# A two-layer transformer on one core: the transfers of the turned maxima are issued by ScalarE instead of SyncE

## The reference

```
xn = layernorm(x);  x = x + attention0(xn) + ffn0(xn)     # layer 0
xn = layernorm(x);  x = x + attention1(xn) + ffn1(xn)     # layer 1

scores = q k^T      (32 heads of 16 columns, causal, -inf above the diagonal)
weights = softmax(scores * 0.25);  context = weights v;  attention = context Wo + bo
ffn(x)  = (act(x gate_w) * (x up_w)) down_w               # 1792 wide, then 1376 wide
```

## Time and profile before

| | |
|---|---|
| median of 3 runs | 811.23 us (810.88 to 814.6) |
| the profiled execution | 813.03 us, of which 811.1 us are the span from its first to its last instruction |
| granted TensorE clock, mean | 0.993 |
| PE, PEld | 769.3 us (95%), 589.6 us (73%) |
| DVE, ACT, POOL | 520.8 us (64%), 406.4 us (50%), 403.7 us (50%) |
| DMA | 113.79 MB, 55.3% of 16 engines' span, all issued by SP (669 issues, 128 of them for the maxima) |
| chain that ended last | PE 79%, DVE 7%, DMA 6%, SP 4%, issue 2%, ACT 2% |

### The profile page before, as it was taken

How to read it: one execution, slowest core, us unless ns; L and a number is a source line. 1 busy time by engine, 2 the same in 40 slices (tenths; PEclk the granted TensorE clock), 3 DMA queues, 4 the chain that set the end, 5 groups by cost and what they waited for, 6 DMA issues and landing times.

```text
span 811.1 us, 19165 instructions
## 1 busy us (share of the span) xinstructions
PE 769.3 (95%) x7172; PEld 589.6 (73%) x7172; DVE 520.8 (64%) x1536; ACT 406.4 (50%) x756; POOL 403.7 (50%) x549
## 2 busy tenths in 40 slices
PE   7899999999999999999979989997989989999996
PEld 4788888877777876687657767674766767787764
DVE  7777765677765678766578668515776857765323
ACT  2253455466655556545535564452364635645630
POOL 4344555555755554455435544357454644555631
PEclk9999999999999999999999999999899999999999
DMA  6557347463736363637784373289628586833331
GB/s 220 135 190 165 116 145 159 115 150 101 159 110 141 117 142 108 141 103 155 206 159 161 87 149 100 68 194 216 168 100 166 157 173 195 150 118 108 96 103 66
DMA packets 71932, 113.79 MB, mean 140 GB/s; under 512 B 21144, under 2 KB 21144, under 8 KB 71832
## 3 DMA queue, kind: packets, MB, share of 16 engines
q1 hardware_dynamic: 71840, 112.57, 55.3%
HBM read 87.04 MB, written 25.43 MB: 139 GB/s over the span
## 4 chain that ended last, share of the span: by engine, by line
PE 79%; DVE 7%; DMA 6%; SPq 4%; issue 2%; ACT 2%; POOL 0%; DVEq 0%; ACTq 0%
PE bank L1347 63%; PE bank L1491 6%; PE bank L1475 4%; PE bank L1457 4%; SPq L940 3%; DMA w_raw<-weights_in 2%; DVE bank L1292 2%; DMA k_op<-qk_scratch 1%; DMA m_scratch<-m_rows 1%; DMA q_op<-m_scratch 1%; DVE gate L1254 1%; DVE xt_lo L1221 1%; ACT gate L1099 1%; PE bank L1367 1%; DMA x<-x_in 1%
## 5 line engine op out<-in xcount | busy, mean ns | idle before, releaser
L1045 POOL TENSOR_TENSOR w_lo<-w_raw,w_hi 128x512 fp32r<-128x512 f32 x202 | 264.2, 1319 | 124.6 <-ACT w_hi L1087 122.0
L1292 DVE CUSTOM_DVE_ANT_0 bank<-bank,causal 128x128 f32<-128x128 f32 (+3 forms) x512 | 237.0, 520 | 76.1 <-PE bank L1457 75.3
L1067 POOL TENSOR_SCALAR_AFFINE_SELECT p<-p 128x256 f32<-128x256 f32 (+1 forms) x320 | 118.2, 370 | 256.5 <-ACT p L1080 248.9
L1080 ACT ACTIVATE p<-bank 128x512 f32<-128x512 f32 x320 | 173.6, 597 | 119.2 <-PE bank L1475 118.7
L1347 PE MATMUL bank<-xt_hi,w_hi 64*128 64x512 f32 x1008 | 206.0, 400 | 13.5 <-DVE h L1263 4.8
L1347 PE MATMUL bank<-xt_lo,w_hi 64*128 64x512 f32 x1008 | 201.6, 391 | 0.0
L1347 PE MATMUL bank<-xt_hi,w_lo 64*128 64x512 f32 x1008 | 201.3, 391 | 0.0
L1087 ACT ACTIVATE w_hi<-w_raw 128x512 fp32r<-128x512 f32 x202 | 120.8, 631 | 33.5 <-DMA w_raw<-weights_in 17.0
L1347 PEld LDWEIGHTS bank<-xt_hi,w_hi 64*128 64x128 f32 x1008 | 98.4, 187 | 38.8 <-DVE h L1263 6.2
L1347 PEld LDWEIGHTS bank<-xt_hi,w_lo 64*128 64x128 f32 x1008 | 98.3, 187 | 18.6
L1347 PE MATMUL bank<-w_hi,h_hi 64*128 64x512 f32 x528 | 108.8, 405 | 3.1 <-ACT p L1080 1.4
(11 more groups left out here) (74 smaller groups left out, 700.6 us busy)
## 6 DMA issues: line engine op xcount, KB each, us to landing
w_raw<-weights_in SPq DMA_DIRECT2D x202, 256.0 KB, 3.1
qk_scratch<-qk_parts SPq DMA_DIRECT2D x24, 512.0 KB, 3.6
q_op<-qk_scratch SPq DMA_DIRECT2D x96, 128.0 KB, 4.7
o_scratch<-o_t SPq DMA_DIRECT2D x32, 256.0 KB, 3.1
k_op<-qk_scratch SPq DMA_DIRECT2D x48, 128.0 KB, 7.7
context<-o_scratch SPq DMA_DIRECT2D x16, 256.0 KB
inverse<-r_scratch SPq DMA_DIRECT2D x16, 256.0 KB
k_op<-k_scratch SPq DMA_DIRECT2D x48, 64.0 KB, 5.2
```

What stands on the lines that cost most here:

```text
L1045: pool.tensor_tensor(w_lo[:, c % SPLIT, :], w_raw[:, c % RAW, :], w_hi[:, c % SPLIT, :].bitcast(F32), ALU.subtract).then_inc(split_done, 1)
L1067: pool.affine_select(out=view, in_=view, compare_op=ALU.is_ge, fill=0.0, base=0, pattern=[[0, n], [1, P]] if n == 2 else [[1, P]], channel ...
L1080: act.activation(p32[:, j % PRING, :], bank_of(g)[:, :], ACT.Exp, scale=SCALE).then_inc(exp_done, 1)
L1292: last = dve.tensor_tensor_reduce(out=bank[:, at:at + n], in0=bank[:, at:at + n], in1=causal[:, 512 - n:], scale=1.0, scalar=LOWEST, op0=A ...
```

## The change

`mout` and `min` leave SP's list and stand in ACT's: the same transfers, waits and semaphores, issued by the other engine. The plan gets two costs for them on ACT (0.5 and 0.3 us), and places a `min` 1.0 us later after its `mout` than before (`ROWS_LATER`). Since the plan has other costs, some steps of PE, DVE and POOL change places with neighbours too.

```diff
--- before.py
+++ after.py
@@ -85,7 +85,7 @@
 
 PE_US = {"xtr": 0.75, "proj": 2.76, "v0": 2.7, "v1": 1.38, "out": 1.38, "S": 0.25, "T": 0.25, "PV": 2.8, "busy": 2.5}
 ACT_US = {"whi": 0.53, "root": 1.6, "root2": 1.6, "xhi": 0.55, "qhi": 0.59,
-          "tanh": 0.5, "exp": 0.5, "oev": 0.5, "hhi": 0.53}
+          "tanh": 0.5, "exp": 0.5, "oev": 0.5, "hhi": 0.53, "mout": 0.5, "min": 0.3}
 DVE_US = {"stats": 3.2, "rstd": 1.1, "ms": 0.6, "rstd2": 1.2, "xn": 0.55, "xlo": 0.7, "qres": 0.68,
           "vsum": 0.62, "gsum": 0.61, "hmul": 0.61, "xadd": 0.62, "smax": 0.67, "mrow": 0.6,
           "recip": 0.45, "norm": 0.75, "hlo": 0.7}
@@ -99,6 +99,7 @@
 O_WRITE, O_READ = 4.0, 8.0
 R_WRITE, R_READ = 4.0, 5.0
 BIAS_READ = 8.0
+ROWS_LATER = 1.0
 
 
 EARLY = 4.0
@@ -475,7 +476,7 @@
         free_pair(n, done)
         if i == VISITS - 1:
             done = end["mrow", u] = place("dve", max(done, after("mout", u - 2)), "mrow", u)
-            done = end["mout", u] = place("sp", max(done, after("min", u - 2)), "mout", u) + TRANSFER
+            done = end["mout", u] = place("act", max(done, after("min", u - 2)), "mout", u) + TRANSFER
             end["min", u] = NEVER
             if u < 4 or at("T", u - 4) < NEVER:
                 rows_load(u)
@@ -484,7 +485,7 @@
 
     def rows_load(u):
 
-        end["min", u] = place("sp", max(end["mout", u], after("T", u - 4)), "min", u) + TRANSFER
+        end["min", u] = place("act", max(end["mout", u] + ROWS_LATER, after("T", u - 4)), "min", u) + TRANSFER
 
     def trans_ready(v):
 
@@ -951,24 +952,6 @@
                             rows = ROW_TILE * half + g * HD
                             sp.dma_start(k_op[rows:rows + HD, octet % 2, 0:2, :].bitcast(F32), group[part]
                                          ).then_inc(k_here[octet % 2], 16)
-                elif kind == "mout":
-                    u = s[1]
-                    sp.wait_ge(smax_done, n_smax[(u,)])
-                    if u >= 2:
-                        sp.wait_ge(m_here[u % 2], 32 * (u // 2))
-                    for part in range(2):
-                        sp.dma_start(m_scratch[u % 2, part].rearrange("r (i t) -> i r t", i=4),
-                                     m_rows[:, u % 2, part, :].bitcast(F32)).then_inc(m_out[u % 2], 16)
-                elif kind == "min":
-                    u = s[1]
-                    sp.wait_ge(m_out[u % 2], 32 * (u // 2 + 1))
-                    if u >= 4:
-                        sp.wait_ge(t_made, t_count(u - 4))
-                    p0 = 2 * (u % 2)
-                    for half in range(2):
-                        rows = ROW_TILE * half + QROWS
-                        sp.dma_start(q_op[rows:rows + 2, u // 2 % 2, p0:p0 + 2, :].bitcast(F32),
-                                     m_scratch[u % 2][:, 8 * half:8 * half + 8, :]).then_inc(m_here[u % 2], 16)
                 elif kind == "oout":
                     u = s[1]
                     octet = u // 2
@@ -1134,6 +1117,24 @@
                     src = h if what == "d" else context
                     act.activation(h_hi[:, hs % HSPLIT, :], src[:, tile, :], ACT.Copy
                                    ).then_inc(hhi_done, 1)
+                elif kind == "mout":
+                    u = s[1]
+                    act.wait_ge(smax_done, n_smax[(u,)])
+                    if u >= 2:
+                        act.wait_ge(m_here[u % 2], 32 * (u // 2))
+                    for part in range(2):
+                        act.dma_start(m_scratch[u % 2, part].rearrange("r (i t) -> i r t", i=4),
+                                     m_rows[:, u % 2, part, :].bitcast(F32)).then_inc(m_out[u % 2], 16)
+                elif kind == "min":
+                    u = s[1]
+                    act.wait_ge(m_out[u % 2], 32 * (u // 2 + 1))
+                    if u >= 4:
+                        act.wait_ge(t_made, t_count(u - 4))
+                    p0 = 2 * (u % 2)
+                    for half in range(2):
+                        rows = ROW_TILE * half + QROWS
+                        act.dma_start(q_op[rows:rows + 2, u // 2 % 2, p0:p0 + 2, :].bitcast(F32),
+                                     m_scratch[u % 2][:, 8 * half:8 * half + 8, :]).then_inc(m_here[u % 2], 16)
                 elif kind == "root":
                     _, l, b = s
                     act.wait_ge(stats_done, n_stats[("stats", l, b)])
```

## The result

The changed kernel takes 839.92 us, median of 4 runs (838.14 to 840.46), against 812.91 us for the kernel before on the same chip (median of 4). The ratio is 1.032, with a 95% interval of 1.029 to 1.034: 3.2% slower. The forecast was 813.5 us with a range up to 822; it was wrong in size, and its range did not hold the time.

What follows compares the result with a forecast made beforehand. PE, busy 769.3 of 811.1 us, was taken as the bound. 813.03 + 6.75 (ACT's stops) - 4.5 (T's waits) gave 815.3 us for the profiled execution; from the median, 811.23 + 2.25, about 813.5 us, range 806.5 to 822.

Steps and rivals of the forecast that it cites:

- The landing on ACT's queue, 2.6 to 3.5 us: `mout` issued from ACT's own queue would land in 2.6 to 3.5 us, within bounds of 2.6 and 9.0.
- The gain of 4.5 us at T: At units 15 and 16, PE's two waits of T for `min` would go: 4.5 us gained, between 0 and 4.5.
- `ROWS_LATER` keeps `min` about 3.5 us behind `mout`: In ACT's list, this spacing exceeds the 2.6 us landing, so ACT should not stand for it at most units.
- The stops for `mrow`: ACT reaching `mout` before `mrow` is done, and issuing, delays PE: five main places and four smaller, 6.75 us, bounds 3 to 16.
- Unit 12: `mout` ahead of unit 11's `oev` on ACT delays the bank PE's projection needs, slack 0: cost 2.8 us.
- Unit 1: `mout` between two `exp` on ACT delays the second, then POOL's mask and `wlo`, which PE needs: cost 0.85 us.
- Unit 24: `mout` ahead of an `exp` pair on ACT delays T of the next visit, which waits for that pair: cost 0.9 us.
- Unit 26: Behind `mout` on ACT an `hhi` comes 1.2 us later, delaying PE's product of 648.00: cost 1.1 us.
- Order, 0 ±2 us: Other order changes swap neighbours on PE with the same work: cost 0, bounds -2 and +2 us.
- Clock, nothing: PE stays at nearly full clock, since stops of 1 to 3 us did not bring it down: nothing added.
- SP's relief, 0 to 2 us: Weights issued earlier by SP gain little, as its largest wait, for a raw buffer, stays: 0 taken, bounds 0 and 2.
- Rival 2: Small transfers are held up on ACT's queue too, stopping ACT 6.4 us at unit 15: 824 us, chance 12%.

Runs made afterwards that it cites:

- e7: The changed kernel with three quarters of the large `q_op` (from octet 2) and `k_op` (from octet 10) reads left out; ratio to the kernel before 0.9995.
- e3: The changed kernel's plan and orders, but SP instead of ACT issues `mout` and `min` at the planned times; ratio to the kernel before 1.009.
- e8: e3 plus 16, 20 and 8 unread matmuls on PE ahead of T's waits at units 16, 24 and 29; ratio to the kernel before 1.006.
- e12: The changed kernel, with SP standing from each `mout`'s planned time until it has landed, issuing nothing; ratio to the kernel before 1.018.
- e1: The changed kernel with `min` given back to SP and `mout` left on ACT, under its own plan; ratio to the kernel before 1.011.
- e2: The changed kernel with `mout` given back to SP and `min` left on ACT, under its own plan; ratio to the kernel before 1.012.
- e6: e3 plus 128 same-size transfers issued by ACT at the `mout` and `min` places, without waits before the program's end; ratio to the kernel before 1.010.

## Why the prediction was wrong, step by step

- *The landing on ACT's queue, 2.6 to 3.5 us.* This is the step that failed. The bounds were 2.6 and 9.0, and the near end was taken because "what stands ahead" in SP's queue was thought to be the difference. At unit 15 it was 9.1 us, at or past the far end; at units 16, 19, 22 and 29 it was 6.0 to 7.9. The reads delay a `mout` that has a queue of its own just as well, as e7 shows by shortening them.
- *The gain of 4.5 us at T.* It was to follow from this step and fell with it. The waits at units 15 and 16 grew from 4.5 to 8.6 us, a loss of 4.1 where 4.5 was to be gained.
- *"`ROWS_LATER` keeps `min` about 3.5 us behind `mout`", so that ACT doesn't stand.* Wrong with the same number: ACT stood some 28 us before `min`, 6.3 at unit 15, 3.7 at 16, 6.6 at 22, some 4 at 29.
- *The stops for `mrow`.* Two of five were sized rightly. Unit 12: 2.8 forecast, 2.77 measured, ended by `o_t` as told. Unit 1: 0.85 and 0.88, with PE starting 0.1 us after the end of the `wlo` named. Unit 24: 0.9, and T waited 0.50 for `exp`. Unit 26: 1.1 more was forecast for the product that began at 648.00 in before, behind a wait of 0.66; in after this is the one at 665.30, and it waited 0.41, so nothing was paid. Unit 25: 0.7, and there was no wait. PE in after at units 1, 24 and 26:

```profile
96.71 0.51 PE L1348 MATMUL bank<-xt_hi,w_hi 64*128 64x512 f32 x2 [0.88 <-issue]
...
623.55 0.50 PE L1458 MATMUL bank<-k_op,q_op 48*128 48x512 f32 x2 [1.09 <-DVE maxima L1293]
624.55 0.50 PE L1476 MATMUL bank<-q_op,k_op 50*128 50x256 f32 x4 [0.50 <-ACT p L1063]
...
665.30 0.50 PE L1348 MATMUL bank<-w_hi,h_hi 64*128 64x512 f32 x2 [0.41 <-issue]
...
669.71 0.50 PE L1348 MATMUL bank<-w_hi,h_hi 64*128 64x512 f32 x2 [1.04 <-DVE h_lo L1271]
```

- *Order, 0 ±2 us.* e3 puts it at 0.9%, some 7 us. The neighbours that change places are equal in work but not in what they wait for. The waits of 1.09 for the maxima and 1.04 for an `h_lo` above belong here and not to ACT's stops: e3, where ACT issues nothing, has them too, and before has neither. T's waits for the landing grew by 8.3 us, and there is half clock behind them, as e8's windows show. From e3:

```profile
607.60 0.50 PE L1462 MATMUL bank<-k_op,q_op 48*128 48x512 f32 x2 [1.09 <-DVE maxima L1297]
...
659.88 0.49 PE L1352 MATMUL bank<-w_hi,h_hi 64*128 64x512 f32 x2 [1.44 <-DVE h_lo L1275]
```

- *Clock, nothing.* "Stops of 1 to 3 us did not bring it down" was true of the two rows it rested on, and the change made stops of 4.5, 4.1 and 3.2 us. In the two traces some 9 us of the 25.1 are this; against a usual execution of before, at 0.988, it is less. The prediction had named it as what would break the forecast, without a price.
- *SP's relief, 0 to 2 us.* Its sign was missed. Weights did come a little sooner (ACT waited 13.1 us for them, before 17.0), but an SP that stands had a use: e12, which puts it back, is 1.3% faster than after.
- *Rival 2* was the mechanism, with its place (unit 15, a stop of 6.4 us; measured 6.3) and its condition (a landing of over 5 us). It had 12% and 824 us. It fell short by 16 us because it put 6 us on all the stops, counted no half clock behind them, and took SP's traffic to stay as it was.

What stays open: the step that failed is known, and that the reads are behind it, but not what holds the first packet back. What is left after e12, 1.8%, less the order's 0.9%, is 0.9%, which should hold the `mrow` stops (unit 12's 2.77 us is in e12 too) and the landings that e12 didn't shorten; no run parts them. Nor is it shown why the halves e1 and e2 don't add up.

## What to carry to other kernels

Before a transfer's issue moves to an engine that also computes, list what it waits for: the issue is cheap (here 76 us of it, in e6, cost nothing that could be told), the wait stands in the compute list and holds up whatever frees the next engine's buffers. Take the landing time at its worst place, behind the largest burst of any queue, and don't count a second queue as a way past it unless a trace shows one. A wait of a transfer engine beside its own small transfer may be what keeps part of a burst away; look at what it will issue once it no longer waits.

## What the runs showed of the hardware that was not expected

- A pair of 16 KB writes on a queue of its own began to move 5.1 to 5.9 us after its issue, while the other queue moved 0.8 to 1.3 MB; at best it was 1.2 us.
- An issue costs ACT what it costs SP: the medians over 64 of each, in after, stand beside the earlier trace rows with 532 and 258 ns.

```profile
L1126 ACTq DMA_DIRECT2D m_scratch<-m_rows x64: 512/526/1092, 76.2 to 764.7; - x64
...
L1136 ACTq DMA_DIRECT2D q_op<-m_scratch x64: 228/266/381, 80.3 to 767.9; - x64
```

- The same gap doesn't always bring the clock down. After the 2.8 us of unit 12 the clock was 1.00 in after, and 0.50 in e12. After:

```profile
324.00:330.00 6.00, 6.00 (x54) 4.83 (x54) 2.53 (x7) 1.95 (x4) 1.69 (x4) 1.00 0.39 135
```

and e12:

```profile
323.00:329.00 6.00, 5.32 (x26) 4.14 (x28) 1.87 (x6) 1.57 (x3) 0.87 (x2) 0.50 0.46 139
```

So the price of such a gap here was 2.8 us in the one, and in the other 3.4 us more (half of the 6.8 us at half clock).
